# Attention block with ternary feed-forward on one core: the feed-forward weights' place, the early scores' grouping and one reciprocal are moved

## The chip, the core and the metric

The kernel runs on one core of a Trainium2 chip. The time is device microseconds of one execution. The engines are named as the profile names them: PE is TensorE's matmuls and PEld its weight loads, DVE is VectorE, ACT is ScalarE, POOL is GpSimd, SP is SyncE, whose queue here issues all transfers.

## What is computed

```python
def _L0_attn_ref(x, w_q, w_k, w_v, w_o):          # x: (2, 1024, 512), 32 heads of 16
    q, k, v = (proj(w_q), proj(w_k), proj(w_v))
    scores = jnp.einsum('bhqd,bhkd->bhqk', q, k) / jnp.sqrt(jnp.float32(D_K))
    attn = jax.nn.softmax(scores, axis=-1)
    out = jnp.einsum('bhqk,bhkd->bhqd', attn, v)
    ...
def bitlinear(x, w, scale):
    w_mean = jnp.mean(jnp.abs(w))
    w_q = jnp.clip(jnp.round(w / (w_mean + EPS)), -1.0, 1.0)
    w_eff = w_q * w_mean * scale
    return jnp.einsum('...i,oi->...o', x, w_eff)
def _L0_ffn_ref(x, w_gate, w_up, w_down, s_gate, s_up, s_down):     # 512 -> 1376 -> 512
    xq = int4_quant(x)
    gate = bitlinear(xq, w_gate, s_gate)
    up = bitlinear(xq, w_up, s_up)
    gate = jnp.square(jax.nn.relu(gate))
    inter = int8_quant(up * gate)
    return bitlinear(inter, w_down, s_down)
x = x + _L0_attn_ref(_layernorm(x, axis=-1), L0_attn_w_q, L0_attn_w_k, L0_attn_w_v, L0_attn_w_o)
x = x + _L0_ffn_ref(_layernorm(x, axis=-1), L0_ffn_w_gate, L0_ffn_w_up, L0_ffn_w_down, ...)
```

A weight is made ternary in steps: the mean of its absolute values over the whole matrix, a division by it, rounding, and a clip to -1, 0 or 1. Each of the three feed-forward weights is handled in four quarters of 128 x 1376 or 128 x 1408 elements.

## The kernel before

There are 2048 tokens in 16 tiles of 128. The program has three phases, and each engine's order is written out by hand; the engines meet only at semaphores.

**Early phase.** x is normalised on DVE (`dve_bn`, `dve_stats`, `dve_normalise`; the inverse deviations come from `rstds` on POOL), transposed on PE, and kept as a high and a low float16 part (`act_tile_copy`, `dve_tile_rest`). Then PE runs six *jobs* (`pe_job`, 12 matmuls each: projections of q or k for one group of heads). ACT copies a job's result out of PSUM, POOL splits it (`pool_split_job`), and SP writes the two halves to HBM and reads them back stacked (`sp_parts_out`, `sp_stack_k`, `sp_stack_q`). After that comes the *values phase*: per tile four times (three matmuls of the values projection, L307, and one score *item*, L365). A score item is a 128x512 block of scores with 48 rows of contraction; consecutive items alternate between rows 0 to 47 and rows 64 to 111 (`item_of`: `side = 1 - k % 2`). DVE takes a row maximum of each item (`dve_max`, L930). Three PSUM banks hold items, so item n waits for the maximum of item n-3. In the same phase the gate and up weights are loaded, summed by ACT (`act_abs`, L640), rounded by ACT (`act_round`, L648) and clipped by DVE (`dve_ternary`, L917 and L919). The first score item waits for the stacked k and q; the first value matmul waits for `dve_weights(2)`, which stands in DVE's queue behind the normalisation of tiles 8 to 11.

**Attention.** Eight *superunits* of four *units* of eight *steps*; a unit has 32 score items. In each step PE computes four score items for the unit two ahead (L365), four transposed score blocks of the present one (L401) and the weighted sum of the step before (`pe_av`, L422); ACT takes four exponentials (L660) and DVE four maxima. Units 0 to 25 also carry one job, two matmuls a step from r = 2 on (r is the step in the unit, `at` the unit). `pe_max_rows` needs POOL's `pool_split_max` and comes at r = 1.

**Last superunit and tail.** In superunit 7, steps 16 to 31 have no score items left, so DVE has no maxima. There the down weight is summed on ACT, and rounded and clipped on DVE. `dve_reciprocal(0)`, the softmax denominators of the first batch, stands at step 8 of it and waits for a transfer that SP issues behind the loads of the down weight, x and the output weight (`sp_tail_loads`). The tail is the output projection and the feed-forward per tile.

```python
                if last and step == 8:
                    dve_reciprocal(dve, 0)
```

## Time and profile before

| what | us |
|---|---|
| runs shown (3) | 1103.1 to 1108.71, median 1107.39 |
| the profiled execution | 1107.77, its span 1106.0 |
| PE busy | 993.5 (90%) |
| DVE busy | 862.5 (78%) |
| ACT busy | 779.8 (71%) |
| POOL busy | 139.8 (13%) |

The busy shares are averages over the phases: the early phase ends at about 150 us, the attention at about 897 us. PEclk in the profile is the granted clock of TensorE: 1.0 is 2.4 GHz and 0.5 is 1.2 GHz.

### The profile page before, as it was taken

How to read it: one execution, taken by the hardware profiler on the slowest of the kernel's cores; microseconds unless marked ns; L12 is line 12 of the kernel's file. 1: busy time of each engine (PE TensorE's matmuls, PEld its weight loads, DVE VectorE, ACT ScalarE, POOL GpSimd, SP SyncE). 2: the span in 40 equal slices, each digit the busy share in tenths (PEclk: the TensorE clock that was granted, in tenths of full speed). 3: DMA queues.
4: the chain of work that ended last, by engine and by line, in shares of the span. 5: the costliest groups of instructions: out<-in, count | busy, mean ns of one | idle time of the engine just before them, and what ended most of it. 6: DMA issues, size and time to landing. Idle time of an engine off the chain costs nothing.

```text
span 1106.0 us, 16495 instructions
## 1 busy us (share of the span) xinstructions
PE 993.5 (90%) x5789; PEld 278.5 (25%) x5806; DVE 862.5 (78%) x1544; ACT 779.8 (71%) x1404; POOL 139.8 (13%) x285
## 2 busy tenths in 40 slices
PE   5478999999999999999999999998878979999997
PEld 3122222222222222222221222221111114444443
DVE  6187579888889888988889888999963227878874
ACT  5344248888888888888888888888858525766665
POOL 3400000110102101111012010110000011112110
PEclk9879899999999999999999999999978568999999
DMA  9510011102101111111110210211453023111001
GB/s 358 177 51 1 1 29 34 35 26 71 40 21 48 48 41 49 35 41 46 51 35 20 63 54 20 50 44 35 133 189 87 9 91 91 48 39 57 21 20 39
DMA packets 37993, 64.90 MB, mean 59 GB/s; under 512 B 3606, under 2 KB 18966, under 8 KB 37654
## 3 DMA queue, kind: packets, MB, share of 16 engines
q1 hardware_dynamic: 37910, 63.85, 19.4%
q8 instruction: 46, 0.75, 0.3%
q14 instruction: 37, 0.30, 0.1%
HBM read 42.27 MB, written 21.23 MB: 57 GB/s over the span
## 4 chain that ended last, share of the span: by engine, by line
PE 67%; DVE 12%; ACT 10%; issue 7%; DMA 2%; SPq 1%; POOL 0%; ACTq 0%; POOLq 0%; DVEq 0%
PE ps L422 18%; PE ps L365 15%; DVE mx L930 9%; PE ps L401 8%; PE ps L343 8%; PE ps L463 5%; PE ps L307 5%; PE ps L486 4%; PE ps L510 3%; ACT PB L660 2%; ACT OS L666 1%; ACT nmT L671 1%; ACT PB L738 1%; DMA qk<-att_d 1%; ACT XV L716 1%
## 5 line engine op out<-in xcount | busy, mean ns | idle before, releaser
L930 DVE TENSOR_REDUCE mx<-ps 128x1 f32<-128x512 f32 x1024 | 644.7, 684 | 91.5 <-PE ps L365 91.2
L660 ACT ACTIVATE PB<-ps 128x512 f32<-128x512 f32 x1024 | 560.1, 595 | 146.5 <-PE ps L401 140.3
L365 PE MATMUL ps<-QK 48*128 48x512 f16 x1024 | 304.6, 389 | 34.4 <-DVE mx L930 34.1
L401 PE MATMUL ps<-QK 50*128 50x512 f16 x1024 | 299.8, 396 | 5.7 <-ACT PB L660 4.6
L422 PE MATMUL ps<-PB,Vg 128*32 128x512 f32 x2048 | 287.5, 635 | 0.7 <-ACT PB L660 0.7
L365 PEld LDWEIGHTS ps<-QK 48*128 48x128 f16 x1024 | 77.7, 93 | 392.9 <-DVE mx L930 303.8
L343 PE MATMUL ps<-XV,wqk 128*128 128x512 f16 x384 | 111.7, 387 | 14.1 <-ACT nmT L671 14.1
L1161 POOL TENSOR_SCALAR nmb<-nm 128x16 f16<-128x16 f32 x32 | 6.6, 205 | 630.8 <-DVE nm L935 630.8
L401 PEld LDWEIGHTS ps<-QK 50*128 50x128 f16 x1024 | 58.5, 95 | 43.9 <-ACT PB L660 42.2
L422 PEld LDWEIGHTS ps<-PB,Vg 128*32 128x32 f32 x2048 | 41.0, 110 | 110.7 <-ACT PB L660 95.5
L463 PE MATMUL ps<-wo,XV 128*128 128x512 f32 x128 | 60.2, 614 | 1.6 <-DVE wqk L960 0.9
L307 PE MATMUL ps<-PB,XV 128*128 128x512 f16 x192 | 60.2, 428 | 1.5 <-ACT XV L595 1.5
L960 DVE TENSOR_TENSOR wqk<-ps,wqk 128x512 f32<-128x512 f32 x16 | 11.1, 692 | 54.0 <-PE ps L463 54.0
L605 ACT ACTIVATE XV<-ps,vback 128x512 f32<-128x512 f32 x16 | 11.0, 687 | 52.6 <-PE ps L307 52.6
L486 PE MATMUL ps<-tu,Vg 128*128 128x512 bf16 (+1 forms) x190 | 45.8, 362 | 1.6 <-DVE XV L1004 1.5
L486 PE MATMUL ps<-tg,Vg 128*128 128x512 bf16 (+1 forms) x191 | 46.0, 363 | 1.1 <-ACT Vg L707 1.1
L343 PEld LDWEIGHTS ps<-XV,wqk 128*128 128x128 f16 x384 | 25.0, 98 | 85.9 <-issue 56.9
L724 ACT ACTIVATE XV<-XV,magic,hm 128x1376 f32<-128x1376 f32 x16 | 24.5, 1533 | 26.5 <-DVE hm L1024 26.5
L510 PE MATMUL ps<-td,PB 128*128 128x512 bf16 (+1 forms) x162 | 39.8, 392 | 2.2 <-ACT PB L738 1.4
L1004 DVE TENSOR_TENSOR XV<-ps,XV 128x512 f32<-128x512 f32 (+1 forms) x48 | 30.2, 630 | 14.2 <-ACT XV L719 12.3
L716 ACT ACTIVATE XV<-ps,agu 128x512 f32<-128x512 f32 (+1 forms) x48 | 30.8, 641 | 12.9 <-PE ps L486 12.8
L1149 POOL TENSOR_TENSOR spl<-qk,spl 128x512 f16<-128x512 f32 x32 | 37.1, 1160 | 6.2 <-POOL spl L1139 6.2
(133 smaller groups left out, 652.8 us busy)
## 6 DMA issues: line engine op xcount, KB each, us to landing
parts_d<-spl SPq DMA_DIRECT2D x64, 128.0 KB
att_d<-OS SPq DMA_DIRECT2D x32, 256.0 KB
QK<-parts_d SPq DMA_DIRECT2D x48, 128.0 KB, 4.7
QK<-parts_d SPq DMA_DIRECT2D x16, 256.0 KB, 4.4
wqk<-x SPq DMA_DIRECT2D x16, 256.0 KB, 6.7
XV<-att_d SPq DMA_DIRECT2D x2, 2048.0 KB, 8.5
QK<-rden_d SPq DMA_DIRECT2D x8, 512.0 KB, 7.7
out<-PB SPq DMA_DIRECT2D x16, 256.0 KB, 2.0
```

What stands on the lines that cost most here:

```text
L307: last = nc.tensor.matmul(ps[:, 4 + t % 2, :], xparts[t // BT][:, a, k, t % BT * P:(t % BT + 1) * P], wv[:, b, k, :], start=(k == 0 and m ...
L343: last = nc.tensor.matmul(ps[:, job_bank(n), :], wqk[:, qk, a, k, group * P:(group + 1) * P], xparts[sup // SPB][:, b, k, half * HALF:(hal ...
L365: nc.tensor.matmul(ps[:, at % S_BANKS, :], QK[rows, sup % 2, 2 * set_ + p, 0, half * HALF + qt * P:half * HALF + (qt + 1) * P], QK[rows, s ...
L401: nc.tensor.matmul(ps[:, T_BANK + n % T_BANKS, :], QK[rows, sup % 2, 2 * set_ + p, 1, kt * P:(kt + 1) * P], QK[rows, sup % 2, 2 * set_ + p ...
L422: last = nc.tensor.matmul(ps[32 * h:32 * h + 32, av_bank(at), :], Vg[:, set_, kt, h, :], PB[:, (sup * STEPS + step) % 3, h, :], start=(kt ...
L463: last = nc.tensor.matmul(ps[:, 0, :], att[:, t % 2, g, :], wo[:, g, :], start=(g == 0), stop=(g == SPB - 1))
L486: last = nc.tensor.matmul(ps[:, bank + n % 2, 0:width], xqT[:, t % 2, k, :], w[:, k, at:at + width], start=(k == 0), stop=(k == KT - 1))
L510: last = nc.tensor.matmul(ps[:, 7, :], qiT[0:n, t % 2, k, :], td[0:n, k, :], start=(k == 0), stop=(k == IT - 1))
L660: nc.scalar.activation(PB[:, at % 3, 2 * (i % 2) + i // 2, :], ps[:, T_BANK + n % T_BANKS, :], ACT.Exp, scale=exp_reg).then_inc(probs, 1)
L716: nc.scalar.activation(rel[:, n % 2, 0:width], ps[:, 2 + n % 2, 0:width], ACT.Relu, scale=agu[:, t % 2, 0:1]).then_inc(rel_ready, 1)
L930: nc.vector.tensor_reduce(mx[:, v % 2, idx, kh:kh + 1], ps[:, at % S_BANKS, :], AX.X, ALU.max).then_inc(s_used, 1)
L1149: nc.gpsimd.tensor_tensor(spl[:, s, 1, :], qk32[:, s, :], spl[:, s, 0, :], ALU.subtract).then_inc(job_split, 1)
```

## The change

The gate and up weights are no longer loaded at the start; all sixteen tiles of x are loaded at once. Each feed-forward weight is now loaded, summed on ACT, averaged, and rounded and clipped in mid-attention: gate in units 13 to 18, up in 18 to 23, down in 23 to 28. All rounding and clipping is done by POOL, three instructions a quarter, two quarters a unit, in units 17, 18, 22, 23, 27 and 28. ACT's twelve sums stand in units 14, 15, 19, 20, 24 and 25 after steps 3 and 6. In units 16, 21 and 26 PE has the mean's matmul at the end of step 2, the job's matmuls begin one step later with three in steps 3 and 4, and DVE has the total before step 0 and the factor before step 3.

In the values phase six value matmuls are followed by two score items. The transposes of tiles 8 to 15 come two at a time before value tiles 4 to 7 (before: four at a time before tiles 8 and 10). DVE normalises tiles 8 to 11 between the first maxima, no longer ahead of `dve_weights(2)`; POOL's inverse deviations for them come after job 3's split, not after job 5's. The reciprocal of the last superunit moves from step 8 to step 16.

```diff
-EARLY_TRANSPOSES = {8: 8, 10: 12}
+EARLY_TRANSPOSES = {4: 8, 5: 10, 6: 12, 7: 14}
...
+WEIGHT_LOADS = (13, 18, 23)
+WEIGHT_SUMS = (14, 19, 24)
+WEIGHT_MEANS = (16, 21, 26)
+WEIGHT_ROUNDS = (17, 22, 27)
...
+        def job_pieces(unit, r):
+
+            cuts = (0, 0, 0, 0, 3, 6, 8, 10, 12) if unit in WEIGHT_MEANS else (0, 0, 0, 2, 4, 6, 8, 10, 12)
+            return range(cuts[r], cuts[r + 1])
...
+                    if n - JOBS_AHEAD in WEIGHT_MEANS:
+                        pe.wait_ge(w_step, 3 * WEIGHT_MEANS.index(n - JOBS_AHEAD) + 1)
...
-                if job_in(at) and r >= 2:
-                    for m in range(2 * r - 4, 2 * r - 2):
+                if job_in(at):
+                    for m in job_pieces(at, r):
                         pe_job(pe, job_in(at), m)
...
-                if last and step == 20:
-                    pe.wait_ge(rows_used, UNITS)
-                    pe_mean(pe, 2)
+                if r == 2 and at in WEIGHT_MEANS:
+                    pe_mean(pe, WEIGHT_MEANS.index(at))
...
             for t in range(TILES):
                 if t in EARLY_TRANSPOSES:
-                    for n in range(4):
+                    for n in range(2):
                         pe_tile_transpose(pe, EARLY_TRANSPOSES[t] + n)
                 for k in range(KT):
                     pe_tile_values(pe, t, k)
-                    item = items(1)
-                    if item == 44:
-                        pe_max_rows(pe, 0)
-                if t == 4:
-                    pe_mean(pe, 1)
+                    if k % 2 == 1:
+                        item = items(2)
+                        if item == 44:
+                            pe_max_rows(pe, 0)
...
-                if last and step in (12, 14, 16, 18):
-                    act_abs(act, 2, (step - 12) // 2)
+                if r in (3, 6):
+                    for w in range(3):
+                        if at - WEIGHT_SUMS[w] in (0, 1):
+                            act_abs(act, w, 2 * (at - WEIGHT_SUMS[w]) + r // 6)
...
             act_job(act, 0)
-            act_abs(act, 0, GATE_ORDER[0])
             act_job(act, 1)
-            act_abs(act, 0, GATE_ORDER[1])
+            act_weights(act, 2, 0, HID)
             act_job(act, 2)
-            act_abs(act, 0, GATE_ORDER[2])
-            act_weights(act, 2, 0, HID)
             act_job(act, 3)
...
         def dve_superunit(dve, sup, last):
             for step in range(STEPS):
+                at, r = sup * 4 + step // KEYT, step % KEYT
+                if at in WEIGHT_MEANS:
+                    if r == 0:
+                        dve_total(dve, WEIGHT_MEANS.index(at))
+                    if r == 3:
+                        dve_factor(dve, WEIGHT_MEANS.index(at))
...
-                if last and step == 8:
+                if last and step == 16:
                     dve_reciprocal(dve, 0)
-                if last and step == 20:
-                    dve_total(dve, 2)
-                    dve_factor(dve, 2)
-                if last and step in (23, 25, 27, 29):
-                    dve_round(dve, 2, (step - 23) // 2)
-                    dve_ternary(dve, 2, (step - 23) // 2, (step - 23) // 2)
...
             dve_total_squares(dve, 2)
+            for t in range(8, 12):
+                dve_bn(dve, t)
+            dve_stats(dve, 2)
             dve_scales(dve, 2)
...
-            dve_tiles(dve, 2)
             dve_weights(dve, 2, 0, HID, 3)
...
+        def pool_ternary(pool, w, q):
+
+            if q == 0:
+                own_wait(pool, w_fac, w + 1)
+            own_wait(pool, w_abs, 4 * w + 4)
+            nc.gpsimd.tensor_scalar(raw(w, q), raw(w, q), wrec[:, w:w + 1], MAGIC, ALU.mult, ALU.add).then_inc(w_round[w], 1)
+            own_wait(pool, w_round[w], q + 1)
+            nc.gpsimd.tensor_scalar(ternq(w, q), raw(w, q), MAGIC, 1.0, ALU.subtract, ALU.min).then_inc(w_min[w], 1)
+            own_wait(pool, w_min[w], q + 1)
+            nc.gpsimd.tensor_scalar(ternq(w, q), ternq(w, q), -1.0, 1.0, ALU.max, ALU.mult).then_inc(w_tern[w], 1)
...
+                for w in range(3):
+                    if at - WEIGHT_ROUNDS[w] in (0, 1):
+                        for q in range(2 * (at - WEIGHT_ROUNDS[w]), 2 * (at - WEIGHT_ROUNDS[w]) + 2):
+                            pool_ternary(pool, w, q)
...
-            for job in range(1, JOBS_AHEAD):
+            for job in (1, 2, 3):
                 pool_split_job(pool, job)
             rstds(2)
+            pool_split_job(pool, 4)
+            pool_split_job(pool, 5)
             rstds(3)
...
-        def sp_down_loads(sp):
+        def sp_weight_half(sp, w, h):
+
+            if w == 0:
+                if h == 0:
+                    sp.wait_ge(job_psum, 4 * SPB)
+                else:
+                    sp.wait_ge(vg_ready, 2 * SPB)
+            else:
+                sp.wait_ge(w_tern[w - 1], 2 * h + 2)
...
-            for q in GATE_ORDER:
-                sp.dma_start(raw_g[q], wgT[q * P:(q + 1) * P, :]).then_inc(raw_in[0], 16)
-            sp.dma_start(raw_u.rearrange("p (k n) -> p k n", k=KT), wuT.rearrange("(k p) n -> p k n", p=P))\
-                .then_inc(raw_in[1], 16)
+            tiles(2)
+            tiles(3)
             sp_aux_rows(sp, 0)
-            tiles(2)
             for n in range(2):
                 sp_parts_out(sp, n)
             sp_stack_k(sp, 0)
...
             sp_parts_out(sp, 5)
-            tiles(3)
-            sp.wait_ge(w_tern[0], 4)
             sp_aux_rows(sp, 1)
```

PE from the projections of the early phase on, before; L343 are jobs, L319 a weight's mean, L307 values, L365 score items:

```order
L343 MATMUL ps<-XV,wqk 128x512 x36
L539 MATMUL ps<-srow,ones 128x3
L343 MATMUL ps<-XV,wqk 128x512 x24
L319 MATMUL ps<-wtot,ones 128x1
L307 MATMUL ps<-PB,XV 128x512 x3
L365 MATMUL ps<-QK 128x512
L307 MATMUL ps<-PB,XV 128x512 x3
L365 MATMUL ps<-QK 128x512
```

The same place now; L296 are transposes:

```order
L348 MATMUL ps<-XV,wqk 128x512 x36
L542 MATMUL ps<-srow,ones 128x3
L348 MATMUL ps<-XV,wqk 128x512 x24
L313 MATMUL ps<-PB,XV 128x512 x6
L370 MATMUL ps<-QK 128x512 x2
...
L296 MATMUL ps<-ident,PB 128x128 x8
L313 MATMUL ps<-PB,XV 128x512 x6
L370 MATMUL ps<-QK 128x512 x2
L313 MATMUL ps<-PB,XV 128x512 x6
L370 MATMUL ps<-QK 128x512 x2
```

The mean is gone from between jobs and values, six value matmuls stand together and two score items behind them, and the transposes come in eights (two tiles).

DVE ahead of the first maxima, before; L819 and L827 are statistics, L836 normalisation, L897 the low part of a weight, L917 and L919 the clip, L930 the maxima:

```order
L892 RECIPROCAL vback<-vback 128x1
L819 BN_STATS bst<-PB 128x6 x4
L827 BN_AGGR bag<-bst 128x2 x4
L836 TENSOR_SCALAR PB<-PB,bag,rstd 128x512 x4
L897 SCALAR_TENSOR_TENSOR PB<-wo,wscale,PB 128x2048
L1076 COPY scal<-ps 128x3
L848 TENSOR_REDUCE wtot<-wsum 128x1
```

The same place now:

```order
L861 RECIPROCAL vback<-vback 128x1
L866 SCALAR_TENSOR_TENSOR PB<-wo,wscale,PB 128x2048
L1033 COPY scal<-ps 128x3
L788 BN_STATS bst<-XV 128x6 x4
L866 SCALAR_TENSOR_TENSOR wqk<-tu,wscale,wqk 128x4x256
L885 TENSOR_REDUCE mx<-ps 128x1 x2
L805 TENSOR_SCALAR PB<-XV,bag,rstd 128x512 x2
L885 TENSOR_REDUCE mx<-ps 128x1 x2
L805 TENSOR_SCALAR PB<-XV,bag,rstd 128x512 x2
```

The values weight's low part no longer stands behind the normalisation, which has moved between the maxima.

POOL in units 22 and 23 of the changed kernel; L1133, L1135 and L1137 are the rounding and the two clips, L1110 to L1116 the split of the maxima, L1088 and L1098 that of a job:

```order
L1133 TENSOR_SCALAR XV<-XV,wrec 128x1376
L1135 TENSOR_SCALAR tu<-XV 128x1376
L1137 TENSOR_SCALAR tu<-tu 128x1376
L1133 TENSOR_SCALAR XV<-XV,wrec 128x1376
L1135 TENSOR_SCALAR tu<-XV 128x1376
L1137 TENSOR_SCALAR tu<-tu 128x1376
L1110 TENSOR_SCALAR nmb<-nm 128x8x2
L1112 TENSOR_SCALAR nmr<-nmb 128x16
L1114 TENSOR_TENSOR nmr<-nm,nmr 128x16
L1116 TENSOR_SCALAR nmb<-nmr 128x8x2
L1088 TENSOR_SCALAR spl<-qk32 128x512
L1098 TENSOR_TENSOR spl<-qk32,spl 128x512
```

Six large instructions stand ahead of the next unit's splits, where before there was none.

## Rows read from the trace of the kernel before

**Rows 1.** The page's forty slices: granted TensorE clock in tenths.

```profile
PEclk9879899999999999999999999999978568999999
```

**Rows 2.** Timeline, PE, early phase: start, us, engine, line, operation, count, [idle before, releaser].

```profile
34.30 5.35 PE L343 MATMUL ps<-XV,wqk 128*128 128x512 f16 x24
59.15 0.59 PE L319 MATMUL ps<-wtot,ones 128*128 128x1 f32 x2 [19.50 <-DVE wtot L848]
...
149.61 0.39 PE L365 MATMUL ps<-QK 48*128 48x512 f16 x2
```

**Rows 3.** Timeline, SP's queue and POOL, 37 to 55 us.

```profile
37.71 1.77 SPq L1297 DMA_DIRECT2D QK<-parts_d  x4
45.14 1.73 SPq L1297 DMA_DIRECT2D QK<-parts_d  x4
53.54 1.02 POOL L1241 TENSOR_TENSOR rstd<-vpe,expo 128x4 f32<-128x4 f32 x1 [0.18 <-POOL vpe L1239]
```

**Rows 4.** DMA issues of the first 180 us: count, KB each, median us to landing.

```profile
QK<-parts_d SPq DMA_DIRECT2D x8, 128.0 KB, 3.4
```

**Rows 5.** Timeline, PE, values phase.

```profile
100.39 1.09 PE L290 MATMUL ps<-ident,PB 128*128 128x128 f32 x8
...
109.50 0.61 PE L365 MATMUL ps<-QK 48*128 48x512 f16 x1
...
111.44 0.61 PE L365 MATMUL ps<-QK 48*128 48x512 f16 x1
...
129.22 0.39 PE L365 MATMUL ps<-QK 48*128 48x512 f16 x1
...
130.29 0.39 PE L365 MATMUL ps<-QK 48*128 48x512 f16 x1
```

**Rows 6.** Timeline, PE, a step in mid-attention.

```profile
505.44 0.48 PE L365 MATMUL ps<-QK 48*128 48x512 f16 x2
```

**Rows 7.** The chain that ended last: start, us, piece; the maxima that follow a unit's end.

```profile
716.94 2.58 DVE mx L930 x4
739.52 1.88 DVE mx L930 x3
...
782.79 1.88 DVE mx L930 x3
```

**Rows 8.** Timeline, ACT and PE around a sum of absolute values, last superunit.

```profile
833.86 1.37 ACT L640 ACTIVATE td<-XV 128x1408 bf16<-128x1408 f32 x1
...
834.61 1.06 PE L422 MATMUL ps<-PB,Vg 128*32 128x512 f32 x8
...
837.64 1.06 PE L422 MATMUL ps<-PB,Vg 128*32 128x512 f32 x8
840.03 1.06 PE L422 MATMUL ps<-PB,Vg 128*32 128x512 f32 x8
```

**Rows 9.** Timeline, POOL and DVE at the start of a unit.

```profile
515.54 0.62 POOL L1139 TENSOR_SCALAR spl<-qk 128x512 f16<-128x512 f32 x1
516.34 1.16 POOL L1149 TENSOR_TENSOR spl<-qk,spl 128x512 f16<-128x512 f32 x1 [0.18 <-POOL spl L1139]
...
513.73 4.36 DVE L930 TENSOR_REDUCE mx<-ps 128x1 f32<-128x512 f32 x7
```

**Rows 10.** Timeline, DVE and POOL, first tiles of the tail.

```profile
911.00 1.37 DVE L993 TENSOR_SCALAR XV<-XV 128x512 f32<-128x512 f32 x1
...
910.56 1.53 POOL L1211 TENSOR_TENSOR XV<-XV,QK 128x512 f32<-128x512 f32 x1
```

**Rows 11.** Timeline, DVE, last superunit.

```profile
812.82 1.75 DVE L953 RECIPROCAL qk<-qk 128x256 f32<-128x256 f32 x1 [5.84 <-DMA qk<-att_d]
...
836.76 0.19 DVE L935 TENSOR_REDUCE nm<-mx 128x16 f32<-128x32 f32 x1
```

**Rows 12.** The chain that ended last, last superunit.

```profile
854.99 1.86 PE ps L422 x8
858.68 1.86 PE ps L422 x8
```

More of the change, by code:

```diff
@@ L58 @@
 W_SCALE = 16.0
-GATE_ORDER = (3, 2, 0, 1)
 CHAIN = (1, 0, 2)
@@ L190, in build @@
         ps = ctx.enter_context(nc.psum_tensor("ps", [P, 8, 512], F32))
-        x_in = [sem(f"x_in{r}") for r in range(8)]
+        x_in = [sem(f"x_in{r}") for r in range(TILES)]
         s_in, wo_in = sem("s_in"), sem("wo_in")
-        raw_in = [sem(f"raw_in{w}") for w in range(3)]
+        raw_in = [[sem(f"raw_in{w}_{h}") for h in range(2)] for w in range(3)]
         consts, ident_ok, id_zero = sem("consts"), sem("ident_ok"), sem("id_zero")
@@ L1077, in _ @@
             dve.wait_ge(scal_ok, 1)
-            dve_total(dve, 0)
-            dve_factor(dve, 0)
+            for t in range(12, 16):
+                dve_bn(dve, t)
             dve_weights(dve, 1, 256, 256, 4)
-            dve_ternary(dve, 0, GATE_ORDER[0], 0)
-            dve_ternary(dve, 0, GATE_ORDER[1], 1)
             for k in range(4 * AHEAD):
@@ L1357, in sp_superunit @@
                         sp_rdn_in(sp, 0)
+                for w in range(3):
+                    if at - WEIGHT_LOADS[w] in (0, 1):
+                        sp_weight_half(sp, w, at - WEIGHT_LOADS[w])
             if last:
@@ L1390, in sp_tail_loads @@
             sp_den_in(sp, 0)
-        def sp_down_loads(sp):
+        def sp_weight_half(sp, w, h):
[6 more added lines that the diff above has]
+                sp.wait_ge(w_tern[w - 1], 2 * h + 2)
+            if w < 2:
+                for q in (2 * h, 2 * h + 1):
+                    sp.dma_start(raw(w, q), (wgT, wuT)[w][q * P:(q + 1) * P, :]).then_inc(raw_in[w][h], 16)
+                return
             w = wdT[0:(IT - 1) * P, :].rearrange("(k p) n -> p k n", p=P)
             half = 2 * DQ
-            for s, c0 in ((0, 0), (3, half)):
-                k0, off = c0 // HID, c0 % HID
-                dst, src_k, c = XV[:, s, 0:half], k0, 0
-                if off:
-                    sp.dma_start(dst[:, 0:HID - off], w[:, k0, off:HID]).then_inc(raw_in[2], 16)
-                    c, src_k = HID - off, k0 + 1
-                n = min((half - c) // HID, IT - 1 - src_k)
-                sp.dma_start(dst[:, c:c + n * HID].rearrange("p (k n) -> p k n", n=HID), w[:, src_k:src_k + n, :])\
-                    .then_inc(raw_in[2], 16)
-                c, src_k = c + n * HID, src_k + n
-                if src_k < IT - 1:
-                    sp.dma_start(dst[:, c:half], w[:, src_k, 0:half - c]).then_inc(raw_in[2], 16)
-                else:
-                    sp.dma_start(dst[0:ILAST, c:half], wdT[(IT - 1) * P:, :]).then_inc(raw_in[2], 16)
+            s, c0 = ((0, 0), (3, half))[h]
+            landed = raw_in[2][h]
+            k0, off = c0 // HID, c0 % HID
+            dst, src_k, c = XV[:, s, 0:half], k0, 0
+            if off:
+                sp.dma_start(dst[:, 0:HID - off], w[:, k0, off:HID]).then_inc(landed, 16)
+                c, src_k = HID - off, k0 + 1
+            n = min((half - c) // HID, IT - 1 - src_k)
+            sp.dma_start(dst[:, c:c + n * HID].rearrange("p (k n) -> p k n", n=HID), w[:, src_k:src_k + n, :])\
+                .then_inc(landed, 16)
+            c, src_k = c + n * HID, src_k + n
+            if src_k < IT - 1:
+                sp.dma_start(dst[:, c:half], w[:, src_k, 0:half - c]).then_inc(landed, 16)
+            else:
+                sp.dma_start(dst[0:ILAST, c:half], wdT[(IT - 1) * P:, :]).then_inc(landed, 16)
         @block.sync
@@ L1420, in tiles @@
                 for t in range(4 * j, 4 * j + 4):
-                    if j > 1:
-                        sp.wait_ge(xn_ready, (t - 7 if j == 2 else t - 3))
-                    sp.dma_start(xin(t), xt[:, t, :]).then_inc(x_in[t % 8], 16)
+                    sp.dma_start(xin(t), xt[:, t, :]).then_inc(x_in[t], 16)
             def weights(w):
```

118 lines of the change are left out of this document (33 added, 85 removed).

## The prediction, as it was put on record before the changed kernel ran

> **What bounds the kernel now.** I read the page's slices first, then the timelines of the three places where PE stands still or runs slowly, then the chain of waits.
>
> The clock line [rows 1] shows full speed through mid-attention and dips at both ends. The early dip begins with a hole: PE ends its six jobs at 34.30 + 5.35 = 39.65 us and does nothing for 19.5 us [rows 2]. The releaser named is DVE, but DVE was itself waiting: the normalisation of tiles 8 to 11 needs POOL's inverse deviations, and these stand in POOL's queue behind all six splits and end at 53.54 + 1.02 us [rows 3]. Each split waits for SP's transfers. Behind the normalisation stand the low part of the values weight and the mean, for which PE waits. The values phase then runs to 149.61 us [rows 2].
>
> In mid-attention the chain alternates between DVE's maxima and PE, with a very even beat: a unit with a job takes 739.52 - 716.94 = 22.58 us, one without (782.79 - 739.52) / 2 = 21.64 us, or 2.70 us a step [rows 7]. PE, DVE and ACT are all nearly full there; POOL is not.
>
> In the last superunit the sixteen steps that have maxima take from 782.79 [rows 7] to 836.86 us (the last reduction starts at 836.76 [rows 11]), 54.1 us where two plain units take 43.3. DVE waited 5.84 us at the reciprocal for its transfer [rows 11]. Later the steps take 858.68 - 854.99 = 3.69 us [rows 12], at half clock; one at full clock took 840.03 - 837.64 = 2.39 us [rows 8].
>
> **The early phase.** *Start.* The first value matmul now needs only the values weight's low part and the scales, which DVE reaches at about 34 us since the wait for POOL is gone from in front of them. So six value matmuls follow the jobs at 39.65 us and end at about 41.0 (5.35 / 24 = 0.22 us each [rows 2]). Then the first score pair waits for the stacked k and q. That chain (ACT copy, POOL split, SP out, SP in) was hidden under the old hole. Stacking of k was issued at 37.71 and that of the first half of q at 45.14 us [rows 3], while weights of 5.6 MB filled the queue ahead of them. With these gone the first halves should land some 2.4 us earlier, an estimate: q's reads issued at 42.7 to 44.5, the last one landing about 3.4 us after its issue [rows 4], at 47.4 us. If the queue was not the cause it is 49.8. PE thus stands still for some 6 us instead of 19.5.
>
> *Rate.* A group of three value matmuls and one item takes 130.29 - 129.22 = 1.07 us at full clock [rows 5], of which 4 x 0.22 is matmuls and about 0.2 is the change between 128 rows and 48 rows. Two groups are 2.15 us. In the new block one such change is saved (0.2), and the two items lie on opposite row halves: in attention two neighbouring items take 0.48 us together where one takes 0.39, so the second starts 0.09 after the first [rows 6] and not 0.22, and the next matmul comes as after one item; that saves another 0.2. A block is 1.74 us. Thirty-one blocks are 53.9 us, the first pair 0.3, the transposes 4 x 1.09 = 4.4 [rows 5], the transposed maxima 0.3: 58.9 us. The smaller price, no overlap of items, is 1.95 a block, +6.5 us. Between pairs DVE has two maxima of 0.62 [rows 9], 1.25 of 1.74 us, and per tile 2 x 0.6 for the low parts and 2 x 0.5 for normalising, which the transposes' 1.09 us cover with about 1 us to spare or to lack; ACT loses its sums and roundings and is idle most of the time.
>
> *Clock.* A block at half clock costs 1.74 + 7 x 0.215 = 3.24 us (a group: 111.44 - 109.50 = 1.94 [rows 5]), so 46% of a half-clock stretch is lost. After the old hole it lasted 5 us, after a short one up to 13. I take 5 us: 2.3 lost; 13 would be 6.
>
> End: 47.4 + 58.9 + 2.3 = 108.6 against 149.6 us. **-41.0 us**, between -30 and -45.
>
> **Mid-attention.** *ACT's sums.* One instruction of 1.37 us [rows 8] plus its read-out. The step around the second one of the old kernel took 837.64 - 834.61 = 3.03 us against 2.70, and the next exponentials caught up: 0.33 us each, 12 x 0.33 = 4.0 us. The other end is the whole length, 12 x 1.37 = 16.4. I take 4.0, since rows 8 show the same instruction in the same loop; the jobs fill PE more there than in those steps.
>
> *Means.* Units 16, 21 and 26: five small DVE instructions of at most 0.19 us [rows 11], 0.9; a mean's matmul, at most 0.59 [rows 2], say 0.3; two third job matmuls, 0.44; but the job no longer starts at step 2, where ACT's row copy holds it, which is what a job unit costs over a plain one, -0.94. 0.7 x 3 = 2.1 us. Queued behind the factor are DVE's maxima, for which PE waits; that is why they count whole.
>
> *POOL.* A 128x512 instruction with one input takes 0.62 us, with two 1.16 [rows 9]. Scaled by 1376 / 512 that bounds one of the 36 between 1.67 and 3.12 us. I take 1.67, since all have one tensor input. A unit then gets 3.8 us of splits (from the unit's start at 513.73 to 517.5 [rows 9]) and 6 x (1.67 + 0.18) = 11.1, together 14.9 of 22.58 us: covered, cost nothing. At 3.12 it is 23.6 and the next unit's maxima are split 1 us late, which PE's place for them (end of step 1) still covers. The Trainium skill, GPSIMD Engine Reference, "3.1 Elementwise — side-by-side cycle accounting", gives about 2.6 cycles an element for two inputs, by which an instruction would be about 3.0 us, an estimate by that page, and the unit just full; the sum would stay the same.
>
> *SP.* Its half loads of 1.4 MB each wait for events five units old or for POOL's clips a unit before; nothing is queued long behind them. Cost nothing; if POOL were late, the next stacked job would be.
>
> Sum **+6 us**, between 0 and +18.
>
> **The end.** With the reciprocal at step 16 and the down weight loaded long before, the sixteen steps take 43.3 instead of 54.1 us: **-10.8** (the sums at steps 12 and 14 are in it). What is late next is SP, whose write of the reciprocal now blocks until step 16; its next work is due at step 18, so no cost. The five steps from 837.64 [rows 8] to 854.99 us [rows 12] took 17.35; without sums I give three of them 2.39 and two 3.69 us, as the clock should fall again when PE has only transposed scores and weighted sums: 14.55, **-2.8**. The other eleven stay at 3.69. The tail is unchanged.
>
> -41.0 + 6 - 10.8 - 2.8 = -48.6. The profiled execution took 1107.8, 0.4 above the median: **1059 us**.
>
> **The rivals.**
> *Clock stays up at the end.* Thirteen steps at 2.39 instead of 3.69: another -17, 1042 us. For it: fewer interruptions by ACT. Against: the old steps without sums never got it back [rows 12]. 12%.
> *ACT's sums cost their length and the stacked rows come no earlier.* +12.4 and +2.4: 1074 us; with a long half-clock stretch 1080. For it: PE is fuller in job units. 14%.
> *Half clock through the whole values phase.* 31 x 1.5 + 4.4 - 2.3 = +48.6: 1108 us, no change. For it: the end of attention stayed at half clock for over 40 us with PE rarely idle. Against: the values phase recovered each time. 8%.
> *POOL holds up DVE.* Where a maximum must wait out each POOL instruction, 36 x 1.67 = 60 us, 1119 us; at 3.12, 1171. It makes the kernel slower once an instruction holds DVE for over 48.6 / 36 = 1.35 us, and its place is units 17, 18, 22, 23, 27 and 28. For it: a DVE tensor_scalar took 1.37 us beside a POOL instruction of 1.53 [rows 10]. Against: seven maxima took 4.36 us, 0.62 each, while POOL split a job [rows 9]. 6%. The Trainium skill, SBUF — State Buffer, "SBUF: two separate sides", says that POOL locks out only DVE instructions in a two-port mode or with two SBUF inputs; a maximum reads PSUM. By that rule, the trace agrees.
>
> **How the numbers follow.** Forecast 60%: 1059 us. The range reaches to the first two rivals, 1038 to 1085, and leaves out the last two and some of the edges. A measurement can tell about 0.5% (5.5 us) from no change. Slower: the last rival and nothing else, 0.06. Same: most of the third, 0.07. Faster: 0.87.
>
> **What would show it.** Early: PE's gap behind the jobs is about 6 us and ends at the first score item near 47; blocks of 1.74 us; the last early item near 108. Units 14 to 26 longer by about 0.7 us where ACT sums; POOL's clips 1.4 to 2 us each and maxima still 0.62 beside them. In the last superunit sixteen steps of 2.70, no DVE wait before step 16. Wrong if the clock line shows half speed over the whole values phase, if the first item starts after 55, or if the units with POOL's clips last over 24 us.

## The result and the profile after

The changed kernel took 1058.35 us (median of four executions, 1057.26 to 1058.86), the kernel before 1106.04 us beside it (1103.1 to 1108.71): a ratio of 0.957, with a 95% interval of 0.954 to 0.960. The forecast was 1059 us. The total is right, but three of its terms are not, and their errors cancel.

| piece of the span, us | before | after | change | forecast |
|---|---|---|---|---|
| start to the end of unit 1's maxima | 150.8 | 108.7 | -42.1 | -41.0 |
| from there to the end of unit 29's (782.7, 760.7) | 631.9 | 652.0 | +20.1 | +6 |
| the sixteen steps to the end of unit 31's (836.8, 809.3) | 54.1 | 48.6 | -5.5 | -10.8 |
| from there to the end of the span (1106.0, 1055.5) | 269.2 | 246.2 | -23.0 | -2.8 |
| sum | | | -50.5 | -48.6 |

The table is of the two profiled executions; the medians lie 47.7 us apart. A piece ends where DVE starts the reduction that finishes the 32 maxima of a unit (the tile nm). The first row has luck of the clock in it: in another run with the same early phase (the reciprocal alone, below) unit 1's maxima end at 146.3 us, with 6.8 us at half clock behind the transposes where the profiled kernel before has 13.7. The page after, against [rows 1]: POOL now works in six units of mid-attention, and the clock dips there, but no longer at the end of attention.

```profile
span 1055.5 us, 16530 instructions
PE 957.6 (91%) x5789; PEld 279.0 (26%) x5806; DVE 842.6 (80%) x1516; ACT 765.8 (73%) x1396; POOL 276.2 (26%) x321
POOL 3500020101121010112981059501990011211110
PEclk9899999999999999999989998899999989999999
```

And the shares of the chain that ended last, where POOL is new:

```profile
PE 59%; POOL 12%; ACT 10%; issue 8%; DVE 8%; DMA 1%; SPq 0%; POOLq 0%; ACTq 0%; DVEq 0%
```

**Early.** The timeline of PE (start, us, what, [idle before]), against [rows 2]. The jobs end at 40.0, six value matmuls follow at once, and the hole is 5.53 us instead of 19.5. The reads of the stacked q, for which the first item waits, are issued at 42.97 us (last line), 2.2 us earlier than before [rows 3], and the item comes 3.90 us behind them. Half clock lasts to 51.3 us, one block and a little of the second; the next takes 54.21 - 52.49 = 1.72 us.

```profile
34.69 5.35 PE L348 MATMUL ps<-XV,wqk 128*128 128x512 f16 x24
39.88 1.46 PE L313 MATMUL ps<-PB,XV 128*128 128x512 f16 x6
46.87 0.88 PE L370 MATMUL ps<-QK 48*128 48x512 f16 x2 [5.53 <-issue]
47.68 2.74 PE L313 MATMUL ps<-PB,XV 128*128 128x512 f16 x6
52.49 0.39 PE L370 MATMUL ps<-QK 48*128 48x512 f16 x2
54.21 0.49 PE L370 MATMUL ps<-QK 48*128 48x512 f16 x2
...
42.97 1.73 SPq L1263 DMA_DIRECT2D QK<-parts_d  x4
```

**Mid-attention.** The groups of POOL between 400 and 800 us (line, shapes, count | busy us, mean ns). Rounding (multiply and add) takes 1.42 us; each of the two clipping instructions takes 4.85, well over both bounds that I had drawn from [rows 9].

```profile
L1137 POOL TENSOR_SCALAR tg<-tg 128x1376 bf16<-128x1376 bf16 x4 | 19.4, 4850 | 0.8 <-POOL tg L1135 0.8
L1135 POOL TENSOR_SCALAR tg<-XV 128x1376 bf16<-128x1376 f32 x4 | 19.4, 4850 | 0.8 <-POOL XV L1133 0.8
L1133 POOL TENSOR_SCALAR XV<-XV,wrec 128x1376 f32<-128x1376 f32 x8 | 11.3, 1417 | 0.0
```

The timelines of POOL, DVE and PE around 540 us, in this order. POOL splits one unit's maxima at 520.71 and the next unit's at 547.60: a unit with two ternary quarters asks POOL for 26.9 us, and PE's unit lasts 22.58. So the maxima that DVE finished at 539.98 wait 7.6 us for POOL, and PE stands 4.42 us at their transposes. Behind that wait the granted clock is at half for 10.2 us (546.2 to 556.5), so such a unit costs more than the wait: this one and its neighbour 8.1 us together. DVE meanwhile takes 0.62 us a maximum beside a 4.85 us instruction of POOL, as it did without one.

```profile
520.71 0.21 POOL L1110 TENSOR_SCALAR nmb<-nm 128x16 f16<-128x16 f32 x1
536.13 1.42 POOL L1133 TENSOR_SCALAR XV<-XV,wrec 128x1376 f32<-128x1376 f32 x1
537.73 4.85 POOL L1135 TENSOR_SCALAR tg<-XV 128x1376 bf16<-128x1376 f32 x1 [0.19 <-POOL XV L1133]
542.77 4.85 POOL L1137 TENSOR_SCALAR tg<-tg 128x1376 bf16<-128x1376 bf16 x1 [0.19 <-POOL tg L1135]
547.60 0.20 POOL L1110 TENSOR_SCALAR nmb<-nm 128x16 f16<-128x16 f32 x1
...
539.98 0.19 DVE L890 TENSOR_REDUCE nm<-mx 128x16 f32<-128x32 f32 x1
540.08 4.36 DVE L885 TENSOR_REDUCE mx<-ps 128x1 f32<-128x512 f32 x7
...
549.05 0.59 PE L387 MATMUL ps<-identh,nmb 128*8 128x128 f16 x4 [4.42 <-POOL nmb L1116]
```

**The end.** PE in the steps without maxima, against [rows 8] and [rows 12], and then two windows (busy us, granted clock behind the engines). A step takes 821.58 - 819.19 = 2.39 us all the way, not 3.69.

```profile
819.19 1.06 PE L426 MATMUL ps<-PB,Vg 128*32 128x512 f32 x8
821.26 0.39 PE L405 MATMUL ps<-QK 50*128 50x512 f16 x1 [0.47 <-ACT PB L643]
821.58 1.06 PE L426 MATMUL ps<-PB,Vg 128*32 128x512 f32 x8
...
820.00:830.00 10.00, 8.12 (x55) 1.94 (x51) 0.00 (x0) 8.54 (x17) 2.31 (x2) 1.00 0.59 144
840.00:850.00 10.00, 7.22 (x44) 1.75 (x45) 0.00 (x0) 7.17 (x14) 0.00 (x0) 1.00 0.01 2
```

The end of attention has two outcomes, some 20 us apart, and a kernel can show both from one execution to the next: of the 29 executions of the kernel before that stand beside these runs, 27 took 1097.9 to 1112.7 us and two 1082.2 and 1081.1.

### The profile page after: what moved, and what is told of

It reads as the page before. It is cut to its first block, busy times and chain, and to the rows that moved or that the text cites. A ratio compares the mean times of both kernels' runs of the same rounds, so it can differ in the third digit from the quotient of the medians.

```text
span 1055.5 us, 16530 instructions
## 1 busy us (share of the span) xinstructions
PE 957.6 (91%) x5789; PEld 279.0 (26%) x5806; DVE 842.6 (80%) x1516; ACT 765.8 (73%) x1396; POOL 276.2 (26%) x321
## 4 chain that ended last, share of the span: by engine, by line
PE 59%; POOL 12%; ACT 10%; issue 8%; DVE 8%; DMA 1%; SPq 0%; POOLq 0%; ACTq 0%; DVEq 0%
PE ps L426 15%; PE ps L370 12%; PE ps L348 7%; PE ps L405 7%; DVE mx L885 6%; PE ps L466 5%; PE ps L313 4%; PE ps L489 4%; PE ps L513 3%; ACT PB L643 3%; POOL td L1135 2%; POOL tu L1135 2%; POOL tg L1135 2%; POOL XV L1133 2%; POOL tu L1137 1%
## 5 line engine op out<-in xcount | busy, mean ns | idle before, releaser
L885 DVE TENSOR_REDUCE mx<-ps 128x1 f32<-128x512 f32 x1024 | 644.1, 684 | 109.0 <-PE ps L370 108.7
L370 PE MATMUL ps<-QK 48*128 48x512 f16 x1024 | 292.8, 389 | 30.0 <-DVE mx L885 24.4
L405 PE MATMUL ps<-QK 50*128 50x512 f16 x1024 | 293.8, 386 | 7.3 <-ACT PB L643 6.3
L426 PE MATMUL ps<-PB,Vg 128*32 128x512 f32 x2048 | 276.2, 612 | 0.7 <-ACT PB L643 0.7
L370 PEld LDWEIGHTS ps<-QK 48*128 48x128 f16 x1024 | 74.8, 93 | 370.4 <-DVE mx L885 297.5
L1110 POOL TENSOR_SCALAR nmb<-nm 128x16 f16<-128x16 f32 x32 | 6.6, 205 | 483.7 <-DVE nm L890 483.4
L915 DVE TENSOR_TENSOR wqk<-ps,wqk 128x512 f32<-128x512 f32 x16 | 11.1, 691 | 58.1 <-PE ps L466 58.1
L1182 POOL TENSOR_SCALAR vpe<-bag 128x1 f32<-128x1 f32 x16 | 6.0, 375 | 162.8 <-DVE bag L919 162.8
L313 PE MATMUL ps<-PB,XV 128*128 128x512 f16 x192 | 48.4, 389 | 0.0
```

The lines of the kernel that those rows point to most:

```text
L313: last = nc.tensor.matmul(ps[:, 4 + t % 2, :], xparts[t // BT][:, a, k, t % BT * P:(t % BT + 1) * P], wv[:, b, k, :], start=(k == 0 and m ...
L370: nc.tensor.matmul(ps[:, at % S_BANKS, :], QK[rows, sup % 2, 2 * set_ + p, 0, half * HALF + qt * P:half * HALF + (qt + 1) * P], QK[rows, s ...
L405: nc.tensor.matmul(ps[:, T_BANK + n % T_BANKS, :], QK[rows, sup % 2, 2 * set_ + p, 1, kt * P:(kt + 1) * P], QK[rows, sup % 2, 2 * set_ + p ...
L426: last = nc.tensor.matmul(ps[32 * h:32 * h + 32, av_bank(at), :], Vg[:, set_, kt, h, :], PB[:, (sup * STEPS + step) % 3, h, :], start=(kt ...
L885: nc.vector.tensor_reduce(mx[:, v % 2, idx, kh:kh + 1], ps[:, at % S_BANKS, :], AX.X, ALU.max).then_inc(s_used, 1)
```

## The experiments

The four theories: **Q**, POOL's queue makes the maxima late; **P**, pairs and an early x make the early phase; **R**, the reciprocal's wait put the clock down at the end of attention; **W**, ACT's late sums did. Times are medians over all executions of a kernel.

### Light clips

```
-tensor_scalar(ternq, raw, MAGIC, 1.0, subtract, min)
+tensor_scalar(ternq, raw, MAGIC, 0.0, subtract, add)
-tensor_scalar(ternq, ternq, -1.0, 1.0, max, mult)
+tensor_scalar(ternq, ternq, 1.0, 0.0, mult, add)
```

> The changed kernel, but the two clipping instructions of every ternary quarter on GpSimd are multiply and add instructions of the same shape and types, so that the clipping at -1 and 1 is left out. Theory Q (the price of minimum and maximum on GpSimd fills its queue, and the pieces of the next unit's maxima come late behind it): the two instructions fall from 4.85 us to about 1.4 us each, a unit with two quarters asks GpSimd for some 14 us and no longer 27, TensorE's waits at the transposes of the maxima go (7.2 us in unit 19, 4.3 and 4.5 in units 23 and 24, about 5 in the last superunit), and the time falls by 18 to 21 us to about 1038. Rival T (the 16-bit output is what costs, not the operation): 4.85 us each stays, time 1058. Rival S (the ScalarE sums and the means slow the middle, not GpSimd): the instructions may get short, but the time stays above 1053.

Measured: 1037.99 us (1036.75 and 1039.23). The waits are gone, and POOL is idle again before the next unit's maxima (third line). Behind the first unit of attention the intervals between the ends of units are 22.6 us (21.6 without a job), except three for each weight of 23.0, 23.3 and 22.9 (22.1 for the last, without a job). Those are ACT's sums and the means, about (0.40 + 0.70 + 0.35) = 1.45 us a weight, 4.4 in all. The last sixteen steps take 43.3 us. Interval by interval POOL had cost 8.1 us at the gate weight, 9.0 at up and 5.3 at down (in the last sixteen steps), 22.5 in all. The table's second row shows less, because the first unit of attention took 23.9 us in the kernel before and 22.5 after. That unit varies by the clock (here it took 26.0, with half clock from 111.1 to 121.3 us), and that is most of why the two profiled executions lie 18.6 us apart and not 22.5. Theory Q holds; S falls, and so does T as the whole price. But my reason for the price does not hold, and only one of the two instructions got short: subtract and add, without a minimum, still takes 4.85 us.

```profile
L1135 POOL TENSOR_SCALAR tg<-XV 128x1376 bf16<-128x1376 f32 x4 | 19.4, 4850 | 0.8 <-POOL XV L1133 0.8
L1137 POOL TENSOR_SCALAR tg<-tg 128x1376 bf16<-128x1376 bf16 x4 | 5.3, 1337 | 0.8 <-POOL tg L1135 0.8
...
543.82 0.20 POOL L1110 TENSOR_SCALAR nmb<-nm 128x16 f16<-128x16 f32 x1 [2.71 <-DVE nm L890]
```

### One slow step taken out

```
 tensor_scalar(raw, raw, wrec, MAGIC, mult, add)
-tensor_scalar(ternq, raw, MAGIC, 1.0, subtract, min)
-tensor_scalar(ternq, ternq, -1.0, 1.0, max, mult)
+tensor_scalar(raw, raw, MAGIC + 1.0, MAGIC - 1.0, min, max)
+tensor_scalar(ternq, raw, 1.0, -MAGIC, mult, add)
```

> The changed kernel with the ternary on GpSimd ordered differently, the result the same: multiply and add the rounding constant as before, then one instruction that clips the rounded number between the constant less 1 and the constant plus 1 (minimum, maximum, 32-bit), then one that takes the constant off as multiply by 1 and add its negative. In the runs so far a multiply and add took 1.34 to 1.44 us for a quarter and every other pair of operations 4.85. If the pair of operations sets the price, a quarter costs 1.4 + 4.85 + 1.4 = 7.7 us instead of 11.1, a unit with two quarters asks for 15.4 + 3.8 us, under its 22.58, the waits at the transposes go, and the time is that of the kernel with light clips: 1038. If each minimum and each maximum costs 3.4 us by itself (two in one instruction 8.3), a quarter is 11.1 us as before and the time stays at 1058. If the write of 16-bit from 32-bit costs, 4.85 us fall to the last instruction and about 1.4 to the clip, and the time is again 1038.

Measured: 1035.94 us (1035.26 to 1036.75), against 1082.21 to 1108.12 for the kernel before beside it. The time is as expected, the price is not: no instruction is slow any more. Its groups of POOL:

```profile
L1133 POOL TENSOR_SCALAR XV<-XV,wrec 128x1376 f32<-128x1376 f32 x8 | 11.3, 1417 | 0.0
L1135 POOL TENSOR_SCALAR XV<-XV 128x1376 f32<-128x1376 f32 x8 | 10.7, 1334 | 1.5 <-POOL XV L1133 1.5
L1137 POOL TENSOR_SCALAR tg<-XV 128x1376 bf16<-128x1376 f32 x4 | 5.4, 1340 | 0.8 <-POOL XV L1135 0.8
```

Minimum with maximum takes 1.33 us, and a 16-bit output from a 32-bit input 1.34 with multiply and add. So neither minimum and maximum nor these types are the cause by themselves. What goes with 4.85 us here is the pair of operations: subtract and minimum, maximum and multiply, subtract and add; what goes with 1.33 to 1.44 is multiply and add, and minimum and maximum. A quarter costs 4.1 us instead of 11.1. This version beats both kernels, the changed one by 1058.35 - 1035.94 = 22.4 us, with ranges that lie 20 us apart.

### The clips on VectorE

```
-pool: own_wait(w_round); tensor_scalar(.. subtract, min); own_wait(w_min); tensor_scalar(.. max, mult)
+def dve_clip(dve, w, q):
+    dve.wait_ge(w_round[w], q + 1)
+    tensor_scalar(ternq, raw, MAGIC, 1.0, subtract, min)
+    dve.wait_ge(w_min[w], q + 1)
+    tensor_scalar(ternq, ternq, -1.0, None, max)
+# dve_superunit: at steps 4 and 6 of the units in WEIGHT_ROUNDS and the ones after
```

> The changed kernel with the rounding instruction left on GpSimd and the two clipping instructions of each quarter on VectorE, at steps 4 and 6 of the same unit. VectorE took 0.88 and 0.52 us for them before the change. Theory Q: GpSimd's queue is short again, the waits at the transposes go, 18 to 21 us less, less what VectorE's 12 x 1.4 = 16.8 us cost where its maxima are waited for (it is busy 80% of the span): 1038 if they fit in its gaps, 1054 if none does. Likeliest 1040. Rival S (sums and means): 1056 or more.

Measured: 1048.39 us (1046.85 to 1049.5). The two instructions take 0.87 and 0.52 us, 2.78 in a unit, and the unit takes 24.6 instead of 22.6 (23.7 instead of 21.6 without a job): 2.0 of the 2.78 us show, six times. DVE's gaps in mid-attention cover only 0.8 of them. It beats the changed kernel by 10 us and loses 12.5 to the version above.

### The reciprocal back at step 8

```
-                if last and step == 16:
+                if last and step == 8:
                     dve_reciprocal(dve, 0)
```

> The changed kernel with VectorE's reciprocal back at step 8 of the last superunit. Theory R (the wait of the reciprocal for its transfer is what put the clock down in the kernel before, and it stayed down until the output projection): steps 17 to 31 go from 2.39 back to about 3.69 us, and the time rises by 17 to 25 us to 1075 to 1083. Rival W (the ScalarE sums and VectorE roundings of the down weight in the last superunit kept the clock down, and they are gone here): only the wait of the reciprocal comes back, 0 to 6 us, 1058 to 1064, with steps 17 to 31 at 2.4 us.

Measured: 1059.22 us (1058.89 to 1059.8), with full clock to the end of attention: R falls, as far as this kernel shows it. But here POOL's lateness may have given the transfer its time. So the same edit on the kernel with light clips:

> The kernel with light clips (1038; clipping left out) with the reciprocal at step 8 of the last superunit. GpSimd's late transposes, which in the changed kernel left the transfer of the denominators time, are away here, so VectorE should wait for it some 5 us as in the kernel before. Theory R2 (that wait is where the clock falls, and from there to the output projection it stays down): 5 us of wait and up to 5 more in the sixteen steps, and 17 to 20 us behind them: 1060 to 1068, in all runs or in some. Rival W (ScalarE's down sums and VectorE's roundings kept the clock down): the wait alone, 1041 to 1047, steps 17 to 31 at 2.4 us.

Measured: 1038.22 us (1036.67 to 1041.57). The issue of the read of the denominators on SP's queue and the reciprocal on DVE in this kernel, and then, below the dots, the same issue in the kernel before:

```profile
761.89 0.53 SPq L1331 DMA_DIRECT2D qk<-att_d  x1
772.07 1.74 DVE L908 RECIPROCAL qk<-qk 128x256 f32<-128x256 f32 x1
...
801.21 0.54 SPq L1362 DMA_DIRECT2D qk<-att_d  x1
```

The reciprocal has no wait in its row: the read took at most 772.07 - 761.89 = 10.2 us, where in the kernel before DVE got it at 812.82, 11.6 us after its issue [rows 11], behind five loads of the down weight. Counted from the end of unit 29's maxima, the issue comes after 14.1 us here and after 18.5 there. The sixteen steps take 44.6 us instead of 43.3. **With the down weight handled earlier, the wait is gone without moving the reciprocal; the move was worth 1.3 us of the sixteen steps beside it, and nothing in the medians.** Since no wait arises here, R2 isn't tested by this run.

### The reciprocal alone, in the kernel before

```
-                if last and step == 8:
+                if last and step == 16:
```

> The kernel before with one edit, VectorE's reciprocal at step 16 of the last superunit instead of step 8. Theory R: the wait of 5.84 us goes and the clock stays at 1.0 after it, steps 17 to 31 take about 2.4 us: 10.8 us in the sixteen steps and 20 us behind them, 1075 to 1080. Rival W (sums and roundings of the down weight, all still here): the sixteen steps get shorter, the rest stays at 3.69 us a step: 1095 to 1101.

Measured: 1071.76, 1073.66, 1091.28 and 1091.48 us, median 1082.47, so between the two expectations, because both occur. In the profiled execution (1071.76) the sixteen steps take 43.6 us instead of 54.1. Behind ACT's sum of step 16 the clock falls, but comes back after 3.4 us and stays up: the eight matmuls of a step's weighted sum take 1.93 us and then 1.07.

```profile
827.68 1.93 PE L422 MATMUL ps<-PB,Vg 128*32 128x512 f32 x8
830.97 1.07 PE L422 MATMUL ps<-PB,Vg 128*32 128x512 f32 x8
```

So this edit alone also takes the 5.84 us wait away: either edit is enough. With all of ACT's sums and DVE's roundings still in place, two of four executions keep the clock and two lose it, 19 us later. R is not what decides it: the clock is lost in two executions with the reciprocal moved. The trace of the kernel before says the same, since the half clock behind its wait lasts from 812.3 to 825.9 us and the steps of [rows 8] after it run at full clock. Whether the move changes the odds (two of four keep the clock, against two of 29) so few executions can't tell. W may be a matter of odds.

### Late sums, all four

```
+                if last and step in (12, 14, 16, 18):
+                    activation(XV[:, 0, 2560:3968], XV[:, 0, 2560:3968], ACT.Abs, accum_out=sqsum[:, 2:3])
```

> The kernel with light clips (1038) and, beside it, four more ScalarE sums of absolute values (128 x 1408 numbers, 1.37 us each in the kernel before) at steps 12, 14, 16 and 18 of the last superunit, where the down weight's stood before the change; their results are used by nothing. Theory R2: they cost 0.33 to 1.4 us each where ScalarE is waited for, 1.3 to 5.5 us in all, and the clock stays at 1.0: 1039 to 1043. Rival W: the clock falls in steps 12 to 19 and steps 17 to 31 go to 3.69 us in all or some of the runs: 1055 to 1063.

Measured: 1039.84, 1057.76, 1062.58 and 1062.91 us. The profiled one is a long one. ACT around its third sum (step 16), and windows of 4 us (PE, PEld, DVE, ACT, POOL busy, clock):

```profile
793.81 1.37 ACT L671 ACTIVATE XV<-XV 128x1408 f32<-128x1408 f32 x1
...
790.00:794.00 4.00, 3.22 (x17) 0.76 (x16) 3.00 (x8) 3.67 (x9) 0.83 (x4) 1.00 0.07 23
794.00:798.00 4.00, 2.86 (x17) 0.86 (x17) 0.00 (x0) 4.00 (x8) 0.00 (x0) 0.82 0.04 13
798.00:802.00 4.00, 3.74 (x14) 0.43 (x12) 0.00 (x0) 2.75 (x6) 0.00 (x0) 0.50 0.38 112
```

From 791 us DVE has no more maxima and PE no more items. In the window from 794 us ACT is busy 4.00 of 4.00 us, PE waits for its exponentials and is busy 2.86 us, and at 796.6 us the clock falls to 1.2 GHz. From there a step takes 816.82 - 813.12 = 3.69 us:

```profile
813.12 1.93 PE L426 MATMUL ps<-PB,Vg 128*32 128x512 f32 x8
816.82 1.93 PE L426 MATMUL ps<-PB,Vg 128*32 128x512 f32 x8
```

W holds, in three of four executions, and ACT's sums are enough for it: this kernel has none of DVE's late roundings. In the kernel before the same place shows the same thing: the sums at steps 16 and 18 start at 839.55 and 847.04 us, and the clock falls behind each, at 843.0 for 3.4 us and at 849.8 for 51.2.

```profile
839.55 1.37 ACT L640 ACTIVATE td<-XV 128x1408 bf16<-128x1408 f32 x1
847.04 1.37 ACT L640 ACTIVATE td<-XV 128x1408 bf16<-128x1408 f32 x1
...
840.00:842.00 2.00, 1.48 (x10) 0.25 (x9) 0.00 (x0) 2.00 (x5) 0.00 (x0) 1.00 0.00 0
842.00:844.00 2.00, 1.38 (x7) 0.52 (x7) 0.00 (x0) 2.00 (x5) 0.00 (x0) 0.75 0.03 8
844.00:846.00 2.00, 2.00 (x11) 0.30 (x11) 0.00 (x0) 1.30 (x3) 0.00 (x0) 0.50 0.25 34
848.00:850.00 2.00, 1.35 (x10) 0.18 (x2) 0.16 (x1) 2.00 (x6) 0.00 (x0) 0.96 0.86 251
850.00:852.00 2.00, 1.99 (x10) 0.40 (x10) 0.00 (x0) 1.91 (x4) 0.00 (x0) 0.50 1.00 238
```

### Which of the sums

The same line with `step in (16, 18)` and with `step in (12, 14)`, on the kernel with one slow step taken out.

> The kernel with one slow step taken out of GpSimd's ternary (1036), and two extra ScalarE sums of absolute values (128 x 1408) at steps 16 and 18 of the last superunit, where the maxima have ended; their results are used by nothing. Theory M (with the maxima gone TensorE has only scores and attention-value matmuls for ScalarE's exponentials, and a sum of 1.37 us in front of them is what drops the clock, which then stays down): most runs fall to half clock behind step 16 or 18 and take 19 to 25 us longer, 1055 to 1061, the others 1037 to 1040. Rival A (it takes all four sums): 1037 to 1040 in all runs.

Measured: 1037.27 and 1038.47 us, and 1057.8, 1057.89, 1058.19 and 1059.42.

> The same, with the two extra ScalarE sums at steps 12 and 14 of the last superunit, beside the last maxima. Theory M: TensorE is still kept busy by the score matmuls for the maxima there, the clock stays up in all runs: 1036 to 1039. Rival A2 (any sum of this length near the end drops the clock): 1055 to 1061 in most runs.

Measured: 1038.76 us, six executions from 1036.34 to 1040.02. Two sums behind the last maximum are enough to lose 20 us in four executions of six; two sums beside the maxima never did it in six, and cost 0.3 us where they stand (43.59 against 43.27 us for the sixteen steps; the rest of the 2.8 us between the medians, 1038.76 and 1035.94 on another chip, isn't theirs as far as the traces show). The four sums of the kernel before stand in the same steps, two beside the last maxima and two behind them. Over all kernels: with sums at steps 16 and 18 nine of 14 executions of the edited kernels took the long end (and all four of the kernel with pairs, below), without them none of 36. The 36 without them are judged by their times and mean granted clocks, and nine of them by a trace too. Why an execution with such sums goes one way or the other stays open: the profiled short one has the same sums and ACT as full (4.00 of 4.00 us).

### Single items

```
-                    if k % 2 == 1:
-                        item = items(2)
+                    item = items(1)
```

> The changed kernel with the early scores one by one behind three value matmuls again, instead of two behind six. Theory P (pairs shorten a block of six value matmuls and two items from 2.15 to 1.72 us, at full clock): 32 blocks x 0.43 us = 13.8 us more, 1072. Rival H (with single items TensorE does not get out of the half clock for a long stretch, as in the kernel before, whose values ran at half clock up to 111 us): the values phase starts at 41 us and stays at half clock for tens of us at some 3.3 us a block: 25 us or more on top, 1083 to 1100. Rival N (VectorE's maxima bound the phase either way): under 1062.

Measured: 1071.7 us (1070.48 to 1074.83), as theory P has it. Unit 1's maxima end at 123.9 us instead of 108.7. Of these 15.2 us the 64 groups of 1.07 us against 32 blocks of 1.72 make 13.4; PE also leaves half clock at 56.7 us instead of 51.3, which is the likely rest. The medians differ by 13.35.

### x behind the first parts

```
-            tiles(2)
-            tiles(3)
             sp_aux_rows(sp, 0)
             for n in range(2):
                 sp_parts_out(sp, n)
+            tiles(2)
+            tiles(3)
             sp_stack_k(sp, 0)
```

> The kernel with one slow step taken out (1036), with the loads of x tiles 8 to 15 moved on the queue behind the parts of the first two jobs. They are then issued at some 33 us instead of 9 us and hold the stacking of the keys up by their 5.1 us of issue; the first score item waits for that stack. Theory X (x at once is a part of the earlier start): the first item comes 5 us later, up to 10 us if VectorE's statistics, which now wait for tile 8, hold the value weights and the later jobs up: 1041 to 1047. Rival X0 (hidden): 1036 to 1038.

Measured: 1044.35 us (1044.28 to 1044.58), 8.4 more; theory X, and the cost is DVE's, as its upper case had it. PE now stands still in its jobs, not only behind them. DVE waits for tile 8; the scales stand behind its statistics, ACT's value weight behind the scales, and ACT's copy of a job, for which PE waits, behind that. The first items come at 53.94 us instead of 46.9, again 3.9 us behind the issue of the stacked q (50.01 us). DVE, ACT and PE:

```profile
36.79 2.82 DVE L788 BATCH_NORM_STATS2 bst<-XV 128x6 f32<-128x512 f32 x4 [10.28 <-DMA XV<-x]
40.47 2.00 ACT L622 ACTIVATE PB<-wo,wscale 128x2048 f16<-128x2048 f32 x1 [10.92 <-DVE wscale L847]
43.10 7.94 PE L348 MATMUL ps<-XV,wqk 128*128 128x512 f16 x24 [8.69 <-ACT qk L609]
53.94 0.67 PE L370 MATMUL ps<-QK 48*128 48x512 f16 x2 [1.61 <-issue]
```

### Pairs alone, in the kernel before

```
-                    item = items(1)
+                    if k % 2 == 1:
+                        item = items(2)
```

> The kernel before with one edit, the early scores in pairs behind six value matmuls. Theory P2 (a pair saves only where the clock is full, from about 111 us in the kernel before; matmuls alone set the time at half clock): 18 blocks x 0.43 us = 8 us less, 1095. Rival C (pairs keep TensorE busier and bring the clock up earlier): 14 to 25 us less, 1078 to 1089. Rival N (no gain): 1103.

Measured: 1091.48 us (1091.08 to 1092.6), 11.8 less and between the first two expectations. The first one was built on a wrong reading: the kernel before is at full clock from 75.0 to 105.7 us, and at half only to 64.8, from 71.6 to 75.0 and from 105.7 to 119.4 us, behind a hole. Unit 1's maxima end at 135.9 instead of 150.8 us, or of 146.3 in the other run with the same early phase: the pairs gave 10.4 to 14.9 us here. By the medians they are worth 11.8 us alone and 13.35 in the changed kernel, so most of their gain doesn't depend on the rest of the change.

## Why the prediction was right, and where it was not

**The early phase** held term by term. The first item came at 46.87 us (47.4), a block took 1.72 us (1.74), half clock lasted about 5 us (5), and the last early item came at about 107.3 us (108.6). The size of the whole has some luck in it: against the other trace of the old early phase (146.3 us) it would be -37.6. The experiments split the 42.1 us: 15.2 are the pairs, the other 26.9 the earlier start, of which x at once is 6.6 (unit 1's maxima end at 115.3 us with x behind the parts, at 108.7 without). The weights gone from SP's queue and the normalisation moved behind the values weight weren't tried apart.

**ACT's sums and means** held: 6.1 us forecast, 4.4 measured where nothing else disturbs them, some 3.3 of it the sums (4.0) and 1.1 the means (2.1). SP showed no cost of its own.

**POOL** is the step that failed: "I take 1.67 ... covered, cost nothing". The bound from both sides, 1.67 to 3.12 us, was scaled from [rows 9] by size and by the number of inputs, and the instruction of those rows with one input multiplies and adds. The clips have other operations, which no row showed, and 24 of them took 4.85 to 4.96 us. The text had even worked out that at 3.12 us PE's place would just cover it; with 4.85 for the clips and 1.42 for the rounding the same sum gives 3.8 + 2 x (1.42 + 2 x 4.85) + 6 x 0.18 = 27.1 us, where 26.9 were measured. Its price is 22.5 us, 17.1 in mid-attention and 5.3 in the sixteen steps, and it pushed mid-attention over the forecast's own upper end of +18. The kernel with fast clips, 22.4 us faster by the medians, gives the same. The Trainium skill, GPSIMD Engine Reference, "3.1 Elementwise — side-by-side cycle accounting", whose price is for two inputs, led to an estimate of 3.0 us; the trace has both 1.42 and 4.85 us for one input and one size, so the measurement decides. The rival that had POOL hold up DVE is false at once: the slowing is by the order of POOL's queue, never by contention (0.62 us a maximum [rows 9] and after). That is in line with the Trainium skill, SBUF — State Buffer, "SBUF: two separate sides", by which POOL locks out only DVE instructions in a two-port mode or with two SBUF inputs.

**The sixteen steps.** -10.8 us is exactly what light clips show, 54.1 to 43.3; in the changed kernel POOL's lateness took half of it back. The cause, though, was named too narrowly: the text gave the gain to the reciprocal at step 16 together with the loads, and each of the two edits gives nearly all of it by itself (43.6 and 44.6 us).

**The end** was the second failed step: "the clock should fall again when PE has only transposed scores and weighted sums". It does not fall by that alone: in 36 executions without sums at steps 16 and 18 it was never lost. The argument against the first rival, that the old steps without sums never got the clock back [rows 12], confused not recovering with falling. At half clock PE needs 3.69 us a step and is never idle long, and yet it stayed there for over 40 us; at full clock it stays up too. The clock can come back in such a stretch: it did so after 3.4 us in the kernel before, and fell again behind the second sum; with the reciprocal moved it came back and stayed. In all traces the last eleven steps kept one clock, and ACT's sums before them are what could tip it. That rival (12%) came true: -23.0 against -2.8, 20.2 us, where it had -17. Of the 23.0 about 19.6 are the clock and 3.4 the sums and roundings that are gone, since the old end of attention at full clock (the reciprocal alone, profiled) took 249.6 us against 269.2 and 246.2.

The two failed steps, +22.5 of POOL and -20.2 of clock, cancel. The forecast hit 1059 us by that luck, not by its sum.

## What to carry to other kernels

A price scaled from a row holds for that row's operations only: before work goes to GpSimd, measure the very pair of operations, and look whether the same result can be had from a fast pair (here 4.1 instead of 11.1 us a quarter, 22 us of the kernel). An engine with idle time still delays what stands behind the new work in its queue; compare the work of one beat, not the busy share. And where TensorE waits for another engine in a light stretch, keep extra work off that engine there, and time such a kernel often enough to see both outcomes.
